# Context rows of a cross-attention: given with exchanged axes and centred in place, instead of transposed on TensorE

## The chip, the cores and the metric

The kernel runs on one core of one Trainium2 chip. The metric is the time of one execution on the device in microseconds (us), as a median of several runs. Beside it there is one profiled execution, whose trace gives every row shown here. The host arranges inputs before the launch; that is not in the time.

## The reference

Three layers are added to `x` (4 batches of 128 rows of 512); the change touches the first, an attention of these 128 latents over 2048 context rows per batch:

```python
ctx = layer_norm(context, ln_ctx_g, ln_ctx_b)        # (x - mean) * rsqrt(var + 1e-5) * g + b, over 512 columns
q = lat @ Wq                                         # lat: the latents, normalised in the same way
k, v = jnp.split(ctx @ Wkv, 2, axis=-1)              # 16 heads of 64
k = apply_rope(k, cos, sin)
attn = softmax(clip(q @ k.T * 64 ** -0.5, -11, 11))
out = attn @ v                                       # then @ Wo + bo, added to x
```

A linear attention and a mixture of experts follow. All of it is float32; products are made of high and low parts (hi*hi + hi*lo + lo*hi).

## The kernel before

`prepare` computes the queries of all batches and splits the weights of keys and values into high and low parts, piece by piece (eight pieces, two buffers). It also does the first four of the 64 context row tiles (128 rows each). A barrier ends it. `attend` is a loop over 128 steps t, each for a pair of heads: 32 steps per batch, in four chunks of 512 context rows, eight steps each. The body of one batch is written out once and looped over. Each engine has its own `step(b, t)`, whose order is the order of its queue; semaphores tie the engines together. TensorE's step is: scores of pair t - 4, values of step t, keys of step t (12 products of 512 columns each), and the weighing of the values by the probabilities of pair t - 5. ScalarE copies the scores, splits probabilities and values and takes exponents; VectorE adds scores (L794), rotates keys (L762 to L776) and takes low parts; GpSimd clips (L617) and makes low parts of probabilities (L610), of rotated keys (L629) and of context rows (L156). Rotated keys are copied by DMA from SBUF to SBUF (`store_keys`, L586), four copies every two steps, and the queries of a pair are loaded from DRAM (L528). All of these DMAs are issued by SyncE, in order.

The context rows of a later chunk are prepared on the way, one tile in each odd step (`row_tile_of`). SyncE loads it with rows on partitions (L565). VectorE takes its mean and variance (L107 to L115), GpSimd the power -1/2 (L120), VectorE normalises it (L126), since mean and factor are one number per partition. TensorE transposes its four blocks against an identity (L134) in the middle of the values' products, after waiting for the normalised rows, and writes a bank of PSUM that it shares with the weighed sums. ScalarE scales and shifts the four blocks out of PSUM (L711; in `prepare` VectorE, L142), now with columns on partitions, takes the high part (L149), and GpSimd the low one (L156). Values and keys wait for the low parts. The order of VectorE in an odd step is: rotate, add weighed sums, normalise (L126), take scores (L794), low values (L803), statistics.

## Time and profile before

| | |
|---|---|
| median of 3 runs | 1433.24 us (1431.34 to 1437.6) |
| profiled execution | 1435.82 us |
| its span in the trace | 1434.1 us |
| TensorE busy | 1383.0 us, 96% |
| VectorE busy | 853.2 us, 59% |
| ScalarE busy | 796.5 us, 56% |
| GpSimd busy | 829.8 us, 58% |
| HBM read and written | 132.67 and 16.78 MB |

The span is that of the instructions on the core; the time of the execution has 1.7 us around it. Busy time of TensorE counts the overlapping parts of pipelined products once; the duration of a single product is longer than its place in the queue, so places are read from starts. An idle time in square brackets stands ahead of the instruction named, with what ended it. L12 is line 12 of the kernel, and "q" behind an engine's name means its queue (waits and issues).

### The profile page before, as it was taken

The page shows a single profiled execution, that of the slowest core. Times are in us where ns is not written, and L with a number is a line of the kernel's source. Part 1 is how long each engine was busy: PE and PEld are TensorE (multiplying, and loading weights), DVE is VectorE, ACT ScalarE, POOL GpSimd, SP SyncE. Part 2 cuts the span into 40 slices and gives each one's busy share as a digit, 9 for nine tenths or more (in the row PEclk, how much of TensorE's full clock was granted, in tenths as well). Part 3 has the DMA queues.
Part 4 walks back from the last instruction along what each step waited for, and adds up shares of the span by engine and source line. Part 5 has one row for each costly group of instructions (what it writes and reads, how often), then busy time and mean ns, then how long its engine had stood idle before and what let it go on. Part 6 is the DMA issues. An engine that isn't in the chain of part 4 may idle for free. (4 is left out here: it accounts for less than half of the span.)

```text
span 1434.1 us, 25248 instructions
## 1 busy us (share of the span) xinstructions
PE 1383.0 (96%) x8758; PEld 1131.0 (79%) x8758; DVE 853.2 (59%) x1422; ACT 796.5 (56%) x1237; POOL 829.8 (58%) x721
## 2 busy tenths in 40 slices
PE   5899999999999999999999999999999999999998
PEld 3578888888788888888888888888888666766654
DVE  6356566566565656665565566665556556657554
ACT  3356666666565666665566666666645512446552
POOL 3267767777676777776677776777766343200002
PEclk9999999999999999999999999999999999899999
DMA  6567676667566666756666766766687545469994
GB/s 240 185 114 131 117 133 107 123 121 133 107 124 123 119 125 115 136 113 122 123 119 111 129 118 130 139 110 117 101 187 133 142 147 183 167 236 360 356 354 141
DMA packets 115267, 218.44 MB, mean 152 GB/s; under 512 B 13360, under 2 KB 49200, under 8 KB 108976
## 3 DMA queue, kind: packets, MB, share of 16 engines
q1 hardware_dynamic: 111968, 209.00, 64.9%
q0 software_dynamic: 1280, 4.20, 0.9%
q10 hardware_dynamic: 1872, 3.41, 0.6%
q8 instruction: 77, 1.26, 0.4%
q14 instruction: 70, 0.57, 0.2%
HBM read 132.67 MB, written 16.78 MB: 104 GB/s over the span
## 5 line engine op out<-in xcount | busy, mean ns | idle before, releaser
L610 POOL TENSOR_TENSOR p_parts<-probs,p_parts 128x512 fp32r<-128x512 f32 x256 | 341.3, 1352 | 249.5 <-ACT p_parts L668 249.5
L668 ACT ACTIVATE p_parts<-probs 128x512 fp32r<-128x512 f32 x256 | 147.7, 625 | 239.0 <-PE banks L978 231.1
L794 DVE TENSOR_TENSOR probs<-banks,probs 128x1024 f32<-128x1024 f32 x128 | 156.7, 1224 | 147.6 <-ACT probs L674 147.6
L698 ACT ACTIVATE probs<-probs 128x1024 f32<-128x1024 f32 x128 | 135.8, 1061 | 144.4 <-POOL probs L617 144.4
L930 PE MATMUL banks<-wv_hi,x_hi 128*128 128x512 f32 x512 | 208.5, 407 | 4.8 <-PEq L170 4.8
L931 PE MATMUL banks<-wv_lo,x_hi 128*128 128x512 f32 x512 | 203.0, 396 | 0.0
L945 PE MATMUL banks<-x_hi,wk_hi 128*128 128x512 f32 x512 | 201.8, 394 | 0.0
L932 PE MATMUL banks<-wv_hi,x_lo 128*128 128x512 f32 x512 | 201.7, 394 | 0.0
L947 PE MATMUL banks<-x_hi,wk_lo 128*128 128x512 f32 x512 | 199.6, 390 | 0.0
L946 PE MATMUL banks<-x_lo,wk_hi 128*128 128x512 f32 x512 | 199.3, 389 | 0.0
L974 PE MATMUL banks<-p_parts,v_hi 128*65 128x128 f32 x1024 | 191.7, 224 | 0.0
L978 PE MATMUL banks<-p_parts,v_hi 128*65 128x128 f32 x1024 | 191.1, 223 | 0.0
L976 PE MATMUL banks<-p_parts,v_lo 128*64 128x128 f32 x1024 | 191.0, 223 | 0.0
L617 POOL TENSOR_SCALAR probs<-probs 128x1024 f32<-128x1024 f32 x128 | 153.6, 1200 | 27.5 <-DVE probs L794 19.2
L914 PE MATMUL banks<-queries,keys 128*128 128x256 f32 x1024 | 150.6, 290 | 6.4 <-issue 5.5
L976 PEld LDWEIGHTS banks<-p_parts,v_lo 128*64 128x64 f32 x1024 | 138.8, 136 | 11.8 <-issue 0.6
L974 PEld LDWEIGHTS banks<-p_parts,v_hi 128*65 128x65 f32 x1024 | 139.5, 136 | 5.2 <-issue 0.5
L978 PEld LDWEIGHTS banks<-p_parts,v_hi 128*65 128x65 f32 x1024 | 139.1, 136 | 0.0
L914 PEld LDWEIGHTS banks<-queries,keys 128*128 128x128 f32 x1024 | 130.8, 191 | 7.6 <-issue 5.7
L674 ACT ACTIVATE probs<-banks 128x1024 f32<-128x1024 f32 x128 | 128.9, 1007 | 9.2 <-PE banks L914 8.7
L932 PEld LDWEIGHTS banks<-wv_hi,x_lo 128*128 128x128 f32 x512 | 97.3, 190 | 22.0
L930 PEld LDWEIGHTS banks<-wv_hi,x_hi 128*128 128x128 f32 x512 | 97.9, 191 | 20.3 <-issue 5.6
(296 smaller groups left out, 2682.4 us busy)
## 6 DMA issues: line engine op xcount, KB each, us to landing
queries<-q_scratch SPq DMA_DIRECT2D x256, 128.0 KB, 6.0
keys<-wo_room SPq DMA_DIRECT2D x128, 256.0 KB, 5.6
keys<-turned_odd SPq DMA_DIRECT2D x128, 256.0 KB, 5.6
row_room<-in_ctx SPq DMA_DIRECT2D x64, 256.0 KB, 6.2
wo_room<-in_down SPq DMA_DIRECT2D x10, 1024.0 KB, 8.0
late_room<-in_gate SPq DMA_DIRECT2D x8, 1024.0 KB
gate_raw<-in_up SPq DMA_DIRECT2D x8, 1024.0 KB, 9.8
up_raw<-in_gate SPq DMA_DIRECT2D x7, 1024.0 KB, 9.1
```

The costliest lines, as they stand in the source:

```text
L610: nc.gpsimd.tensor_tensor(p_parts[:, 1, j, :], probs[:, pair % 2, j, :], p_parts[:, 0, j, :].bitcast(F32), ALU.subtract).then_inc(p_lo_rea ...
L794: nc.vector.tensor_tensor(mine, ps_s[:, :, :, 0, :].rearrange("p j i n -> p (j i) n"), mine, ALU.add).then_inc(s_taken, 1)
L914: mm = nc.tensor.matmul(ps_s[:, j, i], keys[:, slot, 2 * (pair % 2) + j, i * P:(i + 1) * P], queries[:, pair % QUERY_SLOTS, j], start=True ...
L930: nc.tensor.matmul(out, x_hi[:, buf, k, cols], wv_hi[:, k, heads], start=(k == 0), stop=False)
L931: nc.tensor.matmul(out, x_hi[:, buf, k, cols], wv_lo[:, k, heads], start=False, stop=False)
L932: mm = nc.tensor.matmul(out, x_lo[:, buf, k, cols], wv_hi[:, k, heads], start=False, stop=(k == KT - 1))
L945: nc.tensor.matmul(ps_k, wk_hi[:, k, cols], x_hi[:, buf, k, :], start=(k == 0), stop=False)
L946: nc.tensor.matmul(ps_k, wk_hi[:, k, cols], x_lo[:, buf, k, :], start=False, stop=False)
L947: mm = nc.tensor.matmul(ps_k, wk_lo[:, k, cols], x_hi[:, buf, k, :], start=False, stop=(k == KT - 1))
L974: nc.tensor.matmul(sums[:, j, :], v_hi[:, i, 2 * m + j, :], p_parts[:, 0, j, cols], start=(i == 0), stop=False)
L976: nc.tensor.matmul(sums[0:DHEAD, j, :], v_lo[:, i, 2 * m + j, :], p_parts[:, 0, j, cols], start=False, stop=False)
L978: mm = nc.tensor.matmul(sums[:, j, :], v_hi[:, i, 2 * m + j, :], p_parts[:, 1, j, cols], start=False, stop=(i == ROW_TILES - 1))
```

## The change

The host gives the context a second time, as `ctx_t`, in tiles whose axes are exchanged: 512 columns on the partitions (four blocks), 128 rows along them. This copy is loaded into `xt`. The rows with rows on partitions are still loaded (`row_in`), for the statistics alone. Mean and factor are now needed as a row of 128 numbers, the same on every partition: SyncE stores `mean_var` (128 partitions by mean and factor) in DRAM (`row_stats`), waits in its queue until it has landed, and loads it back spread over all partitions (`load_spread`). VectorE subtracts the mean and multiplies by the factor in place (`centre_rows`, both inputs in SBUF, the spread row repeated for the four blocks), behind the taking of the scores. ScalarE scales and shifts in place, behind the exponents. TensorE's transposes go, with its waits for them. Statistics are taken two steps earlier than before, and seven tiles are measured in `prepare`, where four are centred. Space is regrouped: `xt` takes two of the three parts of `row_room`, `bo` gets a place of its own under later tensors.

```diff
--- before.py
+++ after.py
...
-def normalise_row_tile(nc, r, dve, tile, slot):
-    wait(dve, r["rstd_ready"], tile + 1)
-    nc.vector.tensor_scalar(r["row_in"][:, slot, :], r["row_in"][:, slot, :], r["mean_var"][:, slot, 0:1],
-                            r["rstd"][:, slot:slot + 1], ALU.subtract, ALU.mult).then_inc(r["row_ready"], 1)
...
-def transpose_row_tile(nc, r, pe, tile, slot):
-    wait(pe, r["row_ready"], tile + 1)
-    wait(pe, r["full_ready"], tile)
-    for k in range(KT):
-        tr = nc.tensor.transpose(r["ps_tr"][:, k, :], r["row_in"][:, slot, k * P:(k + 1) * P], r["ident"][:])
-    tr.then_inc(r["tr_ready"], 1)
...
+def load_turned(nc, r, d, sp, tile, slot, landed):
+    sp.dma_start(r["xt"][:, slot], d["ctx_t"][tile]).then_inc(landed, 16)
+
+
+def load_spread(sp, to, stats, landed):
+
+
+    whose = stats.rearrange("r w -> (r w)").unsqueeze(0).to_broadcast([P, stats.shape[0] * 2])
+    sp.dma_start(to.rearrange("p n w -> p (n w)"), whose).then_inc(landed, 16)
...
@@ -231,8 +210,7 @@
                 sp.dma_start(x_in[:, b, :], d["x"][b]).then_inc(x_landed[b], 16)
             for n, to in (("lat_g", lat_g), ("lat_b", lat_b), ("ctx_g", keep["ctx_g"]), ("ctx_b", keep["ctx_b"])):
                 sp.dma_start(to[:], d[n]).then_inc(small_landed, 16)
-            for i in range(ROW_TILES):
-                load_row_tile(nc, rows, sp, i, i)
+            sp.dma_start(rows_early[:, 0:ROW_TILES], rows["source"][0:ROW_TILES].rearrange("t p d -> p t d")).then_inc(rows["pair_landed"][0], 16)
...
+            def store_stats(first, last, n):
+                sp.wait_ge(rows["rstd_ready"], n + 1)
+                sp.dma_start(d["row_stats"][first:last].rearrange("t p w -> p t w"), row_mv[:, first:last]).then_inc(rows["stat_stored"], 16)
+                sp.wait_ge(rows["stat_stored"], 16 * (n + 1))
+
             load_piece(0)
+            sp.dma_start(rows["xt"], d["ctx_t"][0:ROW_TILES].rearrange("t p k n -> p t k n")).then_inc(rows["spread_landed"], 16)
+            store_stats(0, ROW_TILES, 0)
+            load_spread(sp, spread_early[:].rearrange("p t n w -> p (t n) w"), d["row_stats"][0:ROW_TILES].rearrange("t p w -> (t p) w"), rows["spread_landed"])
             load_piece(1)
             for m in range(PAIRS):
                 if m + 2 < len(pieces):
                     load_piece(m + 2)
+                if m == 0:
+                    sp.dma_start(rows_early[:, ROW_TILES:MEASURED],
+                                 rows["source"][ROW_TILES:MEASURED].rearrange("t p d -> p t d")).then_inc(rows["pair_landed"][1], 16)
                 if m == 1:
                     load_angles(sp, d, keep, 0, 0)
-                if m >= 4 and m < 7:
-                    load_row_tile(nc, rows, sp, m, m - ROW_TILES)
+                    sp.dma_start(rows["row_in"][:, MEASURED % 2], rows["source"][MEASURED]).then_inc(rows["pair_landed"][1], 16)
+                if m == 5:
+                    store_stats(ROW_TILES, MEASURED, 1)
+                    load_spread(sp, rows["spread"][:].rearrange("p t n w -> p (t n) w"), d["row_stats"][ROW_TILES:EARLY].rearrange("t p w -> (t p) w"), rows["spread_landed"])
+                    for tile in range(ROW_TILES, EARLY):
+                        sp.wait_ge(rows["lo_ready"], tile - ROW_TILES + 1)
+                        load_turned(nc, rows, d, sp, tile, tile % ROW_TILES, rows["pair_landed"][tile % 2])
                 sp.wait_ge(q_lo, m + 1)
                 sp.dma_start(d["q_scratch"][m], q_stage[:, m % 2].rearrange("p b w n -> p b (w n)").bitcast(F32)).then_inc(q_stored[m % 2], 16)
+            for i in range(2):
+                sp.wait_ge(rows["pair_landed"][i], PAIR_BASE[i])
+            sp.wait_ge(rows["spread_landed"], SPREAD_BASE)
...
+
+            def rows_variance(first, last):
+                for i in range(first, last):
+                    stat = nc.vector.bn_aggr(row_mv[:, i, :], row_stats[:, i, :])
+                link(stat)
+                nc.vector.tensor_scalar(row_var[:, first:last], row_mv[:, first:last, 1], EPS, None, ALU.add).then_inc(rows["var_ready"], 1)
+
+            def centre_rows(tile):
+                if tile == 0:
+
+                    dve.wait_ge(rows["spread_landed"], 32)
+                mine = rows["xt"][:, tile]
+                for w, op in ((0, ALU.subtract), (1, ALU.mult)):
+                    link(nc.vector.tensor_tensor(mine, mine, spread_early[:, tile, :, w].unsqueeze(1).to_broadcast([P, KT, P]), op))
+                for k in range(KT):
+                    out = nc.vector.tensor_scalar(mine[:, k, :], mine[:, k, :], keep["ctx_g"][:, k:k + 1], keep["ctx_b"][:, k:k + 1],
+                                                  ALU.mult, ALU.add)
+                out.then_inc(rows["full_ready"], 1)
...
-                    tile = row_tile_of(b, t + 5)
+                    tile = row_tile_of(b, t + 3)
                     if tile is not None:
-                        wait(sp, rows["tr_ready"], b * ROWS_OF_BATCH + (tile - 3))
-                        slot = tile % ROW_TILES
-                        sp.dma_start(rows["row_in"][:, slot, :],
-                                     rows["source"][b * ROWS_OF_BATCH + tile]).then_inc(rows["row_landed"][slot], 16)
+                        whole = b * ROWS_OF_BATCH + tile
+                        wait_alone(sp, rows["lo_ready"], whole - 3)
+                        load_turned(nc, rows, d, sp, whole, tile % ROW_TILES, rows["pair_landed"][tile % 2])
+                        if row_tile_of(b, t + 7) is not None:
+                            wait_alone(sp, rows["stats_ready"], whole + 1 - MEASURED)
+                            sp.dma_start(rows["row_in"][:, tile % 2, :],
+                                         rows["source"][whole + 2]).then_inc(rows["pair_landed"][tile % 2], 16)
                     for pair in (t - 3, t - 2):
                         if exists(b, pair) and exists(b, t - 2):
                             load_queries(b, pair)
+                tile = row_tile_of(b, t + 2) if t >= 1 else None
+                if tile is not None:
+                    whole = b * ROWS_OF_BATCH + tile
+                    if not isinstance(whole, int) or whole >= MEASURED:
+                        wait_alone(sp, rows["rstd_ready"], STATS + whole + 1 - MEASURED)
+                        sp.dma_start(d["row_stats"][whole], rows["mean_var"][:, tile % ROW_TILES, :]).then_inc(rows["stat_stored"], 16)
+                        wait_alone(sp, rows["stat_stored"], 16 * (STATS + whole + 1 - MEASURED))
+                        wait_alone(sp, rows["spread_landed"], SPREAD_BASE + 16 * (whole - EARLY))
+                    wait_alone(sp, rows["xt_ready"], 2 * (whole - 1 - ROW_TILES))
+                    load_spread(sp, rows["spread"][:, tile % 2], d["row_stats"][whole], rows["spread_landed"])
...
-                tile = row_tile_of(b, t + 1) if t >= 2 else None
+                tile = row_tile_of(b, t + 3) if t >= 2 else None
                 if tile is not None:
-                    row_tile_power(nc, rows, pool, b * ROWS_OF_BATCH + tile, tile % ROW_TILES)
+                    mine = rows["mean_var"][:, tile % ROW_TILES, 1:2]
+                    wait(pool, rows["var_ready"], b * ROWS_OF_BATCH + (STATS + tile + 1 - MEASURED))
+                    nc.gpsimd.tensor_tensor(mine, rows["var_eps"][:, tile % ROW_TILES:tile % ROW_TILES + 1],
+                                            rows["minus_half"][:, 0:1], ALU.pow).then_inc(rows["rstd_ready"], 1)
...
+                exponents(b, t - SCORE_LAG)
+                rope_high(b, t, 1)
                 tile = row_tile_of(b, t)
                 if tile is not None:
-                    whole = b * ROWS_OF_BATCH + tile
-                    wait(act, rows["tr_ready"], whole + 1)
-                    wait(act, rows["lo_ready"], whole - 1)
+                    mine = rows["xt"][:, tile % ROW_TILES]
+                    wait(act, rows["xt_ready"], 2 * (b * ROWS_OF_BATCH + (tile - ROW_TILES + 1)))
                     for k in range(KT):
-                        out = nc.scalar.activation(rows["x_full"][:, tile % 2, k, :], rows["ps_tr"][:, k, :], ACT.Identity,
+                        out = nc.scalar.activation(mine[:, k, :], mine[:, k, :], ACT.Identity,
                                                    bias=rows["ctx_b"][:, k:k + 1], scale=rows["ctx_g"][:, k:k + 1])
                     out.then_inc(rows["full_ready"], 1)
-                exponents(b, t - SCORE_LAG)
-                rope_high(b, t, 1)
...
+            def centre_rows(b, tile):
+                whole, slot = b * ROWS_OF_BATCH + tile, tile % ROW_TILES
+                if tile >= EARLY:
+                    wait(dve, rows["pair_landed"][tile % 2], landings(b, tile))
+                    wait(dve, rows["spread_landed"], SPREAD_BASE + 16 * (whole + 1 - EARLY))
+                mine = rows["xt"][:, slot]
+                mean, factor = (rows["spread"][:, tile % 2, :, w].unsqueeze(1).to_broadcast([P, KT, P]) for w in range(2))
+                nc.vector.tensor_tensor(mine, mine, mean, ALU.subtract).then_inc(rows["xt_ready"], 1)
+                wait(dve, rows["xt_ready"], 2 * (whole - ROW_TILES) + 1)
+                nc.vector.tensor_tensor(mine, mine, factor, ALU.mult).then_inc(rows["xt_ready"], 1)
...
+            def measure_rows(b, tile):
+                whole, slot, turn = b * ROWS_OF_BATCH + tile, tile % ROW_TILES, tile % 2
+
+                if tile > MEASURED:
+                    wait(dve, rows["pair_landed"][turn], landings(b, tile - 2))
+                n = whole - MEASURED + 1
+                var = rows["mean_var"][:, slot, 1:2]
+                nc.vector.bn_stats(rows["stats"][:, slot, :], rows["row_in"][:, turn, :]).then_inc(rows["stats_ready"], 1)
+                wait_alone(dve, rows["stats_ready"], n)
+                nc.vector.bn_aggr(rows["mean_var"][:, slot, :], rows["stats"][:, slot, :]).then_inc(rows["mean_ready"], 1)
+                wait(dve, rows["mean_ready"], n)
+                nc.vector.tensor_scalar(rows["var_eps"][:, slot:slot + 1], var, EPS, None, ALU.add).then_inc(rows["var_ready"], 1)
...
+                take_scores(b, t - SCORE_LAG)
                 tile = row_tile_of(b, t)
                 if tile is not None:
-                    normalise_row_tile(nc, rows, dve, b * ROWS_OF_BATCH + tile, tile % ROW_TILES)
-                take_scores(b, t - SCORE_LAG)
+                    centre_rows(b, tile)
                 combine(b, t, 1)
                 values_low(b, t - 1)
                 if not last:
                     finish(b, t - VALUE_LAG - 1)
-                tile = row_tile_of(b, t + 2) if t >= 1 else None
-                if tile is not None and t % 2 == 1:
-                    whole = b * ROWS_OF_BATCH + tile
-                    measure_row_tile(nc, rows, dve, whole, tile % ROW_TILES, b * CHUNKS + (tile // ROW_TILES + 1))
-                    wait_alone(dve, rows["stats_ready"], whole + 1)
-                    row_tile_variance(nc, rows, dve, whole, tile % ROW_TILES)
+                tile = row_tile_of(b, t + 4) if t >= 1 else None
+                if tile is not None:
+                    measure_rows(b, tile)
...
-                    tile = row_tile_of(b, pair + VALUE_LAG)
-                    if tile is not None:
-
-                        wait(pe, rows["full_ready"], b * ROWS_OF_BATCH + tile + 1)
...
-                tile = row_tile_of(b, t)
-                if tile is not None:
-
-                    if exists(b, t - VALUE_LAG - 1):
-                        wait(pe, o_added, b * BSTEPS + (t - VALUE_LAG))
-                    transpose_row_tile(nc, rows, pe, b * ROWS_OF_BATCH + tile, tile % ROW_TILES)
...
+    d["row_stats"] = nc.dram_tensor("row_stats", (BATCH * CTX // P, P, 2), F32).ap()
...
-        keep["row_in"] = room[:, 0:2, :].rearrange("p a (t n) -> p (a t) n", n=DIM)
-        keep["x_full"] = room[:, 2, :].rearrange("p (a t n) -> p a t n", a=2, n=P)
+        keep["xt"] = room[:, 0:2, :].rearrange("p a (t k n) -> p (a t) k n", k=KT, n=P)
+        keep["row_in"] = room[:, 2, :].rearrange("p (t n) -> p t n", n=DIM)
...
+        "ctx_t": a["ctx_1024"].reshape(BATCH * CTX // P, P, KT, P).transpose(0, 3, 2, 1),
...
```

## Rows read from the trace of the kernel before

**Rows 1.** The page: busy time, share of the span, instructions of each engine.
```profile
PE 1383.0 (96%) x8758; PEld 1131.0 (79%) x8758; DVE 853.2 (59%) x1422; ACT 796.5 (56%) x1237; POOL 829.8 (58%) x721
```

**Rows 2.** Table by windows: PE, PEld, DVE, ACT, POOL busy, clock, DMA share, GB/s.
```profile
700.00:957.00 257.00, 257.00 (x1834) 223.20 (x1832) 156.96 (x275) 161.89 (x267) 189.64 (x158) 1.00 0.67 122
```

**Rows 3.** TensorE's waits, 57 to 1130 us: sum, times, longest.
```profile
PE banks L134 <- DVE row_room L126: 2.3, 3, 1.1
PE banks L914 <- DMA keys<-wo_room: 0.8, 1, 0.8
```

**Rows 4.** TensorE's timeline, 500 to 532 us: start, us, instructions.
```profile
506.13 1.17 PE L914 MATMUL banks<-queries,keys 128*128 128x256 f32 x8
...
508.53 0.60 PE L134 MATMUL banks<-ident,row_room 128*128 128x128 f32 x4
...
514.52 1.16 PE L914 MATMUL banks<-queries,keys 128*128 128x256 f32 x8
...
522.46 1.16 PE L914 MATMUL banks<-queries,keys 128*128 128x256 f32 x8
```

**Rows 5.** VectorE's timeline, the same stretch.
```profile
506.83 0.55 DVE L126 TENSOR_SCALAR row_room<-row_room,mean_var,rstd 128x512 f32<-128x512 f32 x1
508.49 1.22 DVE L794 TENSOR_TENSOR probs<-banks,probs 128x1024 f32<-128x1024 f32 x1 [1.11 <-ACT probs L674]
...
513.28 0.69 DVE L765 TENSOR_TENSOR turned_odd<-banks,wo_room 128x512 f32<-128x512 f32 x1 [1.89 <-PE banks L947]
...
518.02 0.69 DVE L776 TENSOR_TENSOR turned_odd<-turned_odd 128x512 f32<-128x512 f32 x1
```

**Rows 6.** ScalarE's timeline, the same stretch.
```profile
514.78 1.16 ACT L668 ACTIVATE p_parts<-probs 128x512 fp32r<-128x512 f32 x2 [2.77 <-PE banks L978]
```

**Rows 7.** GpSimd's timeline, the same stretch.
```profile
509.88 1.04 POOL L617 TENSOR_SCALAR probs<-probs 128x1024 f32<-128x1024 f32 x1
...
515.49 2.67 POOL L610 TENSOR_TENSOR p_parts<-probs,p_parts 128x512 fp32r<-128x512 f32 x2 [3.31 <-ACT p_parts L668]
518.27 1.35 POOL L617 TENSOR_SCALAR probs<-probs 128x1024 f32<-128x1024 f32 x1
...
523.43 2.65 POOL L610 TENSOR_TENSOR p_parts<-probs,p_parts 128x512 fp32r<-128x512 f32 x2 [0.33 <-ACT p_parts L668]
```

**Rows 8.** SyncE's queue, the same stretch: DMA issues.
```profile
517.88 5.29 SPq L586 DMA_DIRECT2D keys<-turned_odd  x4
...
524.28 2.81 SPq L528 DMA_DIRECT2D queries<-q_scratch  x4
```

**Rows 9.** Landings: the copy issued at 522.62; L586; L556; then SyncE's longest wait.
```profile
keys<-turned_odd SPq DMA_DIRECT2D x1, 256.0 KB, 6.8
...
DMA to landing us min/median/max: 3.9/5.6/8.9
...
DMA to landing us min/median/max: 1.6/4.3/6.4
...
SPq L556 <- DVE attn L820: 48.2, 12, 4.1
```

**Rows 10.** Before the loop: a window as in rows 2, then timelines of SyncE, VectorE, GpSimd, TensorE.
```profile
0.00:20.00 20.00, 4.81 (x18) 3.92 (x19) 13.54 (x41) 5.71 (x12) 5.16 (x15) 1.00 0.72 263
...
6.92 15.59 SPq L242 DMA_DIRECT2D w_raw<-in_wv  x3
...
24.77 0.69 DVE L372 TENSOR_TENSOR q_stage<-a_ps,q_stage 128x512 fp32r<-128x512 f32 x1 [1.53 <-ACT q_stage L297]
...
28.86 0.69 DVE L372 TENSOR_TENSOR q_stage<-a_ps,q_stage 128x512 fp32r<-128x512 f32 x1 [2.13 <-ACT q_stage L297]
...
14.57 2.08 POOL L120 TENSOR_TENSOR rstd<-var_eps,minus_half 128x1 f32<-128x1 f32 x4 [2.50 <-DVE var_eps L115]
...
53.75 1.05 POOL L120 TENSOR_TENSOR rstd<-var_eps,minus_half 128x1 f32<-128x1 f32 x2 [6.34 <-DVE var_eps L115]
...
55.14 0.77 PE L930 MATMUL banks<-wv_hi,x_hi 128*128 128x512 f32 x1 [4.82 <-PEq L170]
```

102 lines of the change are left out of this document (46 added, 56 removed).

## Prediction

> **What bounds the kernel now.** I read the page's busy shares first: TensorE is busy 96% of the span, no other engine for computing over 60% [rows 1]. A share is a mean over stages, so next the table by windows: in the attention loop TensorE is busy 257.0 of 257.0 us at full clock, with the DMA engines at 0.67 [rows 2]. Then TensorE's own waits from 57 to 1130 us: beside the turns of the batch loop, 2.3 us in three waits of the row transposes for VectorE's normalised rows, 0.8 us for keys [rows 3]. So in the loop (55 to about 1128 us) each us taken from TensorE's queue is a us of the span, as long as nothing else comes late. TensorE's timeline gives the period: scores begin at 506.13, 514.52 and 522.46, so an odd step (with transposes) takes 8.39 us and an even one 7.94 [rows 4]. The stages behind the attention are not touched.
>
> **The change, part by part.**
>
> *Transposes.* Removed: four per row tile, 60 tiles in the loop. The four take 0.60 us by themselves, but overlap their neighbours; what the queue gives back is the difference of the two steps, 8.39 - 7.94 = 0.45 us [rows 4]. 60 x 0.45 = 27.0 us. Bounds: 0.44 (another pair of steps reads the same to 0.01) and 0.60, if nothing of it overlapped; I take 0.45, the direct reading, and hold 26 to 28. Their three waits, 2.3 us, go with them [rows 3]; what is late next behind them is the score's wait for keys, below, so I count 2. Together 29 us. The 16 transposes of the stage before the loop are under other work there and count nothing.
>
> *VectorE in the loop.* Removed per tile: the normalisation, 0.55 us, that stood in the shadow of the wait for ScalarE's copied scores (1.11 us idle behind it). Added, and moved behind the taking of the scores: two operations with both inputs in SBUF. The nearest row is the sum L776, 0.69 us [rows 5]; lower bound is that, upper bound twice it, since one input is repeated over k and read every other element, which no row shows; I take 0.69, for its size and its places are the same. So the odd step has 1.4 to 2.8 us more between taking the scores (ends 509.71) and the next keys (513.28, behind 1.89 us of idle) [rows 5]. With the odd step 0.45 us shorter, 1.4 us fit in the idle time to within 0.1 us; 2.8 would run 1.3 us over into the even step, where the rotation is wanted only about 3.8 us after the step begins, and the scores still find 1.1 us idle. Cost nothing; the cover is that idle time.
>
> *ScalarE.* The four scalings now read SBUF and stand behind the exponentials. ScalarE has 2.77 us of idle before the next split of the probabilities [rows 6]. The centring ends at about 511.3, the scalings 1.5 us later, 1.5 us before ScalarE is wanted. Nothing.
>
> *GpSimd.* It has the same operations. In the even step it is nearly full: 0.33 us idle before the next split [rows 7], and that step isn't shortened. Beside L776, GpSimd's clip takes 1.35 us, without such a neighbour 1.04 [rows 5, 7]: an operation of VectorE with two SBUF inputs holds GpSimd back by 0.31 us. The new ones will do that in the odd step, two times, 0.6 us, where GpSimd has 3.3 us of idle [rows 7]. The Trainium skill (SBUF — State Buffer, Who interferes with whom) says more: such an instruction and a GpSimd one that reads SBUF exclude each other, and the later "fully blocks". The trace's 0.31 us is in line with a short remainder of such a lock, not with a whole one. This makes a part of rival B.
>
> *The queue of SyncE.* This is the part that can turn the sign. New per tile: a load of the turned tile (256 KB, beside the old one), a store of 1 KB in pieces of 8 bytes, a wait in SP's queue until it has landed, and a load that spreads it over the partitions (128 KB). Before, SP issues four key copies from 517.88 to 523.17, then a row tile, then from 524.28 four query loads in 2.81 us [rows 8]. The new wait comes right behind the last key copy, with which it shares the queue. That copy lands 6.8 us after its issue at 522.62; key copies take 3.9 to 8.9, the small stores of attention results 1.6 to 6.4 [rows 9]. I take X = 5.6 us for the store, landing with the last keys at 529.4; bounds 1.6 and 8.9. Queued behind that wait: the spread load, the turned tile and the row tile at about 0.5 us each (four query loads take 2.8, 0.7 each, with two register waits), and the queries, so SP is free at 523.7 + 5.6 + 4.3 = 533.6, once in four periods 1.2 later for the angles. The next keys are due at 517.88 + 15.9 = 533.8: it just fits. Queries landing 6 us behind their issue (531 for the first pair) are in time for 538. More bytes: 384 KB each 15.9 us, 1.5 us at the 263 GB/s that the first 20 us moved [rows 10]; the DMA share goes from 0.67 to some 0.8.
> The keys are the tight end: the last land at 529.4, the scores that need them begin one period behind 514.52, at 530.4: 1.0 us of slack. If the first key copy goes out over about 2 us late, it joins the other three and all come late. In the periods with angles and with stores of attention results (some 30 of 60) I allow 0.1 us on average: 3 us. Bounds 0 and 0.5 us in all 60, 30 us, of which the upper end is a rival.
>
> *Before the loop.* Here the round trip is on the path. Now the bytes up to both first weight pieces, 5.2 MB, land by about 20 us at 263 GB/s. After: the turned tiles (1 MB) come ahead, SP then waits for powers (made at 14.57 now, in one operation about 17 then), for the store (behind 5.8 MB, so 22 us), issues the spread load and only then the second weight piece, now among the issues from 6.92 on [rows 10]. It lands at about 28, its split ends at 30, and the first query split follows, 24.8 before: 5 us late. VectorE then has 1.4 us more per m for four m (two 0.69 operations), which fits into the 2.13 us idle between them [rows 10]; three early measurements move forward. At m = 5 another store and wait stands ahead of the sixth query store: 3 to 5 us, partly beside others; against that the power of two tiles at the end (1.05 us, until 54.8, the last thing before the loop starts at 55.14) goes away [rows 10]. Sum: +5 + 2 to 4 - 1, I take +6.5; bounds 0 (all made up by the 1.5 to 2.1 us idle of each m) and +13 (both trips in full).
>
> **Sum.** 27 + 2 - 3 - 6.5 = 19.5 us less. The profiled execution had 1435.82 us (span 1434.1); its after is 1416.3. The median before is 1433.24, 2.6 us under it, so the median after is 1433.24 - 19.5 = 1413.7 us.
>
> **Rivals.**
> A. *The start hides it.* The idle of each m absorbs the late start and keys stay in time: -29, 1404 to 1406. For it: idle of about 2 us in each of four m. Against: VectorE needs 1.4 of these for itself. Chance 0.12.
> B. *Keys a little late in every period.* SP's order or the longer queue lets the last keys land 0.3 to 0.5 us after they are wanted: 18 to 30 us, of which 3 are in the sum: 1429 to 1441, no change. For it: 1.0 us of slack is all there is. Against: the keys' own issue hangs on ScalarE and GpSimd, whose even step doesn't change. Chance 0.12. A form of it is a full block between the two engines: if each new operation waits out one of GpSimd of 1.3 us, the odd step of VectorE ends some 2.6 us later, the even step of GpSimd and the last key copy about 2 us, 1 us over the slack; in half the periods that is 30 us, 1444. It is the skill's rule named above. It has 0.04 of B's chance, since the trace shows 0.31 us.
> C. *Slower: SP's queue becomes the bound.* Place: the wait for the landing of the 8-byte pieces. SP can be 2.4 us later than worked out before keys pile up, and then 1.0 us more before scores wait: from X = 9.0 us each further us costs 60 us. At X = 10: 1414 + 60 = 1474 us; break-even is at X = 9.3. For it: 128 pieces of 8 bytes to DRAM, which no row shows. Against: no key copy lands later than 8.9, no small store later than 6.4 [rows 9], and around batch ends SP already waits about 4 us at this place, 12 times, while TensorE's waits for keys are 0.8 us in all [rows 3, 9]. Chance 0.11. The Trainium skill (DMA: Bandwidth & Descriptors, Specifications) asks for 512 B or more per piece, below which the engine reads, modifies and writes; it gives no time for 8-byte pieces. By its fixed cost of about 2 us per transfer (section Anatomy of one DMA) the store would be X = 2, and the 3 us for keys would leave the sum: an estimate of 1411.
> That the transposes don't leave TensorE's queue can't be, by the diff.
>
> **Chances.** Forecast 0.65, A 0.12, B 0.12, C 0.11. Range 1403 to 1432: it takes in the forecast's bounds (1413.7 less 3 and 6.5 for a start and keys that cost nothing, 1404; plus 6.5 and some us of keys, 1424) and part of B. About 0.5% (7 us) is what a measurement of this kernel can tell from no change: faster by more (under 1426) 0.79, within 0.09, slower 0.12.
>
> **What would show it.** Both steps of TensorE at 7.94 us; no wait of L914 for keys or queries; the store's landing near 5.6 us and SP through its queries before the next rope halves are ready; TensorE's first L930 at about 61 to 62, not 55; VectorE's new operations at 0.69 us; centring never waiting for the spread load. Wrong if TensorE shows regular waits at L914, or if VectorE's rotation starts late enough that L945 waits.

## The result, and the profile after it

The changed kernel takes 1497.25 us (median, 1491.59 to 1502.6), the kernel before 1432.29 in the same comparison: a ratio of 1.045, 95% interval 1.042 to 1.0481, so slower by 4.5%. The forecast was 1413.7 us, with a range of 1403 to 1432. The profiled execution took 1498.11 us, its span 1495.2.

The span can be cut at two marks: the first matmul of the values ends the start, the first of the output projection ends the attention loop. All kernels of this study, profiled executions, us (tiles of rows in the loop: 60; e7 has one trip more in 57 of them):

| kernel | start | loop | rest | span | median | ratio to before [95%] |
|---|---|---|---|---|---|---|
| before | 55.1 | 1060.0 | 319.0 | 1434.1 | 1432.3 | |
| after | 71.8 | 1105.2 | 318.2 | 1495.2 | 1497.3 | 1.045 [1.042, 1.048] |
| e1_no_wait | 70.1 | 1051.6 | 322.9 | 1444.6 | 1438.8 | 1.003 [1.001, 1.005] |
| e2_no_round_trip | 70.1 | 1033.4 | 319.9 | 1423.4 | 1425.2 | 0.993 [0.990, 0.996] |
| e3_no_turned_load | 70.2 | 1068.8 | 322.8 | 1461.8 | 1459.9 | 1.017 [1.012, 1.022] |
| e4_wait_later | 70.7 | 1052.4 | 317.1 | 1440.2 | 1435.5 | 1.001 [0.999, 1.003] |
| e6_start_and_later | 65.1 | 1052.7 | 320.0 | 1437.8 | 1437.8 | 1.003 [1.001, 1.005] |
| e7_two_trips | 72.8 | 1288.5 | 320.8 | 1682.1 | 1682.8 | 1.173 [1.169, 1.178] |
| e8_reordered | 64.1 | 1041.3 | 320.4 | 1425.8 | 1426.1 | 0.994 [0.992, 0.997] |
| e9_loop_order | 71.9 | 1039.1 | 317.6 | 1428.6 | 1429.3 | 0.995 [0.994, 0.997] |
| e10_wide_pieces | 71.5 | 1043.8 | 319.9 | 1435.2 | 1436.4 | 1.003 [1.000, 1.005] |
| e13_weights_first | 59.9 | 1037.0 | 317.5 | 1414.4 | 1416.6 | 0.987 [0.985, 0.989] |

So of the 61.1 us that the change costs in the profiled executions (65.0 by the medians), 16.7 lie before the loop, 45.2 in it, and -0.8 behind it. A run's ratio is taken to the kernel before as timed beside it on the same chip, at 1434.3 to 1434.7 us for e1 to e13.

The page of the kernel after, busy time of each engine (before: [rows 1]), and the window of the loop (columns as in [rows 2]):

```profile
PE 1372.0 (92%) x8502; PEld 1116.7 (75%) x8502; DVE 952.0 (64%) x1481; ACT 806.8 (54%) x1237; POOL 882.7 (59%) x716
...
700.00:957.00 257.00, 243.06 (x1690) 209.40 (x1689) 174.43 (x279) 155.71 (x254) 193.94 (x151) 0.99 0.74 140
```

TensorE, full in this window before, now idles 13.9 of 257 us, and no other engine took its place: VectorE is busy 174 us of it, GpSimd 194. That looks like a chain of waits, not like an engine that has too much to do; the experiments decide it. TensorE's waits from 57 to 1170 us name their place (engine, tile and line; what released it; us in all, times, longest), against [rows 3]:

```profile
PE banks L965 <- issue: 36.9, 26, 4.1
PE banks L981 <- PEq L145: 20.1, 1, 20.1
PE banks L965 <- DMA keys<-wo_room: 19.3, 14, 2.6
PE banks L965 <- DMA keys<-turned_odd: 5.4, 8, 1.2
```

L965 (L914 before) is the score matmul; L981 is the first matmul of the values, whose one wait is for the barrier that ends the start. A step between two scores without a wait takes some 7.93 us now, odd or even, where the odd one took 8.39 [rows 4]: the transposes are gone. But some 49 of 128 scores wait. "Issue" means that the profile shows no releaser, so it must be read from the timelines. SyncE's queue and the scores of TensorE in one stretch ("..." stands for the loads of `xt`, `row_in` and the angles):

```profile
539.63 0.40 SPq L593 DMA_DIRECT2D row_stats<-mean_var  x1
546.98 0.34 SPq L119 DMA_DIRECT2D spread_rows<-row_stats  x1
...
548.62 2.82 SPq L543 DMA_DIRECT2D queries<-q_scratch  x4
551.55 3.62 SPq L614 DMA_DIRECT2D keys<-turned_odd  x4
555.42 0.39 SPq L593 DMA_DIRECT2D row_stats<-mean_var  x1
563.99 0.34 SPq L119 DMA_DIRECT2D spread_rows<-row_stats  x1
...
565.63 2.82 SPq L543 DMA_DIRECT2D queries<-q_scratch  x4
...
569.89 2.84 SPq L614 DMA_DIRECT2D keys<-wo_room  x4
572.99 0.39 SPq L593 DMA_DIRECT2D row_stats<-mean_var  x1
```
```profile
555.80 1.19 PE L965 MATMUL banks<-queries,keys 128*128 128x256 f32 x8 [1.50 <-issue]
563.75 1.16 PE L965 MATMUL banks<-queries,keys 128*128 128x256 f32 x8
572.66 1.19 PE L965 MATMUL banks<-queries,keys 128*128 128x256 f32 x8 [0.84 <-issue]
```

Two things are to be seen. First, SyncE goes round here almost without a pause of its own: from store to store 15.79 and 17.57 us, of which 7.35 and 8.57 go by until the store's landing lets it issue the spread load; the rest, 8.4 and 9.0 us, are nearly all issues. The four key copies, paced by ScalarE and spread over 5.29 us before [rows 8], go out at 569.89 in 2.84: they had been ready and waited for SyncE. Over the loop the four take 3.2 us (median of 64 sets, 5.3 before). Two steps of TensorE are 15.9 us, so SyncE has no time left where the landing takes over about 7 us. Second, the queries. They are sent behind the wait, the first pair of copies from 548.62 to about 549.9, and these two land 4.8 and 6.3 us after their issue, the later one at about 555.7; the odd score starts at 555.80, 1.50 us after TensorE was free. The next pair, issued from 565.63, is there at about 572.5, and the score starts at 572.66. So "issue" is a wait for queries here. Taken over the loop, odd scores wait 30.1 us in 25 places, even ones, which use a new set of keys, 32.2 us in 24. The landings confirm the split: ahead of each waiting odd score the queries land last, 0.09 to 0.23 us before it starts, with the keys there for over 8 us. Ahead of the waiting even ones the keys land last; only in two of them, with 7.5 us, had they been there for 1.0 and 3.4 us, and the same two scores wait 5.5 us in the kernel before.

SyncE's slack is its own wait at the key copies for ScalarE, which makes them. Its two rows before (57 to 1130 us) and after (57 to 1170 us), 508.8 us in 125 waits against 90.8 in 61:

```profile
SPq L586 <- ACT wo_room L693: 259.6, 61, 11.5
SPq L586 <- ACT turned_odd L693: 249.2, 64, 7.9
```
```profile
SPq L614 <- ACT wo_room L724: 55.0, 30, 7.6
SPq L614 <- ACT turned_odd L724: 35.8, 31, 5.7
```

The landing itself (us from issue, least, median, most) of the store L593, and SyncE's waits for it from 57 to 1170 us (L65 is the helper that waits; where it has no row, the wait stands at the next issue, L119):

```profile
DMA to landing us min/median/max: 4.9/7.5/10.8
```
```profile
SPq L65 <- DMA row_stats<-mean_var: 332.3, 48, 9.7
SPq L119 <- DMA row_stats<-mean_var: 76.7, 9, 10.1
```

SyncE spends 409 us of the span in 57 waits for 1 KB each. In all 57 the store lands behind the last of the four key copies issued ahead of it, by 0.15 to 2.0 us (median 0.77); that copy is issued 0.84 us before the store and takes 7.5 us itself (median).

### The profile page after: what moved, and what is told of

The parts are those of the page before. It is cut to its first block and busy times, and to the rows that moved or that the text cites. A ratio compares the mean times of both kernels' runs of the same rounds, so it can differ in the third digit from the quotient of the medians.

```text
span 1495.2 us, 25506 instructions
## 1 busy us (share of the span) xinstructions
PE 1372.0 (92%) x8502; PEld 1116.7 (75%) x8502; DVE 952.0 (64%) x1481; ACT 806.8 (54%) x1237; POOL 882.7 (59%) x716
## 5 line engine op out<-in xcount | busy, mean ns | idle before, releaser
L638 POOL TENSOR_TENSOR p_parts<-probs,p_parts 128x512 fp32r<-128x512 f32 x256 | 350.1, 1389 | 180.1 <-ACT p_parts L699 179.8
L645 POOL TENSOR_SCALAR probs<-probs 128x1024 f32<-128x1024 f32 x128 | 173.9, 1358 | 89.3 <-DVE probs L824 86.9
L981 PE MATMUL banks<-wv_hi,x_hi 128*128 128x512 f32 x512 | 204.0, 398 | 20.1 <-PEq L145 20.1
L965 PE MATMUL banks<-queries,keys 128*128 128x256 f32 x1024 | 155.3, 296 | 62.7 <-issue 36.9
L965 PEld LDWEIGHTS banks<-queries,keys 128*128 128x128 f32 x1024 | 133.4, 194 | 70.3 <-issue 56.4
L981 PEld LDWEIGHTS banks<-wv_hi,x_hi 128*128 128x128 f32 x512 | 99.1, 194 | 37.4 <-issue 20.9
L131 POOL TENSOR_TENSOR x_lo<-row_room,x_hi 128x512 fp32r<-128x512 f32 x64 | 109.0, 1704 | 16.2 <-ACT x_hi L124 16.2
```

Source lines behind the costliest of these rows:

```text
L638: nc.gpsimd.tensor_tensor(p_parts[:, 1, j, :], probs[:, pair % 2, j, :], p_parts[:, 0, j, :].bitcast(F32), ALU.subtract).then_inc(p_lo_rea ...
L645: nc.gpsimd.tensor_scalar(mine, mine, CLIP / SCALE, -CLIP / SCALE, ALU.min, ALU.max).then_inc(clipped, 1)
L965: mm = nc.tensor.matmul(ps_s[:, j, i], keys[:, slot, 2 * (pair % 2) + j, i * P:(i + 1) * P], queries[:, pair % QUERY_SLOTS, j], start=True ...
L981: nc.tensor.matmul(out, x_hi[:, buf, k, cols], wv_hi[:, k, heads], start=(k == 0), stop=False)
```

## The experiments

Theory (C of the prediction): SyncE's queue, stretched by the wait for the store, is the bound in the loop. Rivals: more bytes to move; VectorE and GpSimd in each other's way (B's lock form); the start alone. The first three kernels each take one thing away, e4 moves one.

**e1_no_wait**: store and spread load stay, the wait is for the store of the tile before, which landed long ago.

```diff
+wait_alone(sp, rows["stat_stored"], 16 * (STATS + whole - MEASURED))
 sp.dma_start(d["row_stats"][whole], rows["mean_var"][:, tile % ROW_TILES, :]).then_inc(...)
-wait_alone(sp, rows["stat_stored"], 16 * (STATS + whole + 1 - MEASURED))
...
-load_spread(sp, rows["spread"][:, tile % 2], d["row_stats"][whole], rows["spread_landed"])
+load_spread(sp, rows["spread"][:, tile % 2], rows["source"][whole][0:1, 0:2 * P], rows["spread_landed"])
...
```

> The changed kernel, but SP doesn't wait for the landing of the mean and factor of this tile (only, ahead of the store, for that of the tile before), and the spread load reads 1 KB of the context instead, so the rows are centred with other numbers: the result isn't the attention's. All DMAs and all work of the engines stay. Theory W (the wait in SP's queue makes queries and keys late): the loop loses its 70 us of waits, about 1430 us; the start, 16.7 us later than before, stays. Theory B (the bytes of the added loads make keys late): 1490. Theory C (VectorE's two operations and GpSimd hold each other up): 1490.

Measured 1438.8 us, the loop 53.6 us shorter than in the changed kernel, with all its bytes and all its work on VectorE and GpSimd. Both of these rivals had 1490. Waits of odd scores: none; even ones still wait 22.7 us in 14 places, so not all of the 70 us went.

**e2_no_round_trip**: in the loop no store, no wait, no spread load.

```diff
-sp.dma_start(d["row_stats"][whole], rows["mean_var"][:, tile % ROW_TILES, :]).then_inc(...)
-wait_alone(sp, rows["stat_stored"], 16 * (STATS + whole + 1 - MEASURED))
-wait_alone(sp, rows["spread_landed"], SPREAD_BASE + 16 * (whole - EARLY))
-load_spread(sp, rows["spread"][:, tile % 2], d["row_stats"][whole], rows["spread_landed"])
...
 (ahead of the turned load)
+wait_alone(sp, rows["xt_ready"], 2 * (whole - 1 - ROW_TILES))
 (VectorE, ahead of the centring)
-wait(dve, rows["spread_landed"], SPREAD_BASE + 16 * (whole + 1 - EARLY))
```

> The changed kernel without store, wait for landing and spread load in the loop: every tile there is centred with the mean and factor of tiles 4 and 5, so the result isn't the attention's. The turned loads and the engines' work stay. Theory W: as the run without the wait, 1425 to 1430 us. Theory B: a third of the added bytes goes, 1475. Theory C: 1490.

Measured 1425.2 us, the loop 1033.4: 26.6 less than before, where 27.0 were forecast for the transposes. The two new operations of VectorE, the four scalings from SBUF and the turned load are all still in it, so together they cost nothing that can be seen. Its window, to be held against [rows 2] and the window above:

```profile
700.00:957.00 257.00, 256.43 (x1814) 222.08 (x1813) 189.97 (x298) 166.31 (x273) 209.70 (x161) 1.00 0.68 143
```

This gives the price of the round trip in the loop: 1105.2 - 1033.4 = 71.8 us. The waits at the scores make 54 us of it (60.9 against 6.8, from the first score on). In the ten windows of 100 us from 100 to 1100 the granted clock is 0.988 on average in the changed kernel and 0.996 here, some 8 us; the last step before a wait shows 8.09 us, the wait itself not counted, where a free one shows 7.93, some 48 times, another 8.

**e3_no_turned_load**: the turned tile isn't loaded, the round trip stays.

```diff
-load_turned(nc, rows, d, sp, whole, tile % ROW_TILES, rows["pair_landed"][tile % 2])
...
 (VectorE, ahead of the centring)
+wait(dve, rows["lo_ready"], whole - 3)
```

> The changed kernel without the turned tile's load in the loop (256 KB less per tile, one issue less); old contents are centred again, so the result isn't the attention's. Store, wait and spread load stay. Theory W: SP's chain is 0.5 us shorter per tile, 1480 to 1490 us. Theory B: two thirds of the added bytes go, 1450. Theory C: 1490.

Measured 1459.9 us, the loop 1068.8, 36.4 us shorter than in the changed kernel. The 1480 to 1490 of the theory is missed, and the time lies nearer to the 1450 of the rival with the bytes. That rival alone doesn't hold, since e1 and e2 carry the same load at 1051.6 and 1033.4 us; but beside the wait the load costs more than the theory said. SyncE has one issue less, some 0.6 us, and the store lands at a median of 6.9 us instead of 7.5; SyncE's waits for it stay the largest (303.3 us in 48, the other form 68.6 in 9). Read as the same closed loop, shorter by these two amounts, 1.2 us in 57 tiles would give up to 68 us, and 36.4 were measured; so the size isn't explained, and which of the two does more wasn't taken apart.

**e4_wait_later**: the same store at the same place, but its wait and the spread load stand behind the queries of the next even step.

```diff
 sp.dma_start(d["row_stats"][whole], rows["mean_var"][:, tile % ROW_TILES, :]).then_inc(...)
-wait_alone(sp, rows["stat_stored"], 16 * (STATS + whole + 1 - MEASURED))
-wait_alone(sp, rows["spread_landed"], SPREAD_BASE + 16 * (whole - EARLY))
...
 (behind load_queries of step t, even)
+tile = row_tile_of(b, t + 1) if t >= 2 else None
+    wait_alone(sp, rows["stat_stored"], 16 * (STATS + whole + 1 - MEASURED))
+    wait_alone(sp, rows["spread_landed"], SPREAD_BASE + 16 * (whole - EARLY))
+    load_spread(sp, rows["spread"][:, tile % 2], d["row_stats"][whole], rows["spread_landed"])
```

> The changed kernel, all of its work kept, but in the loop the wait for the landing and the spread load stand behind the query loads of the next even step instead of right behind the store. The store has the time of the other loads' issues to land. Theory W: most of the 70 us of waits in the loop go, about 1430 us, with the late start left. Theory B: 1490. Theory C: 1490.

Measured 1435.5 us, the loop 1052.4. The store lands no sooner (5.3, 7.4, 9.3), so its time alone costs nothing; what cost was standing ahead of queries and keys. Odd scores wait nowhere now, even ones 22.2 us in 12. TensorE's waits, 57 to 1170 us:

```profile
PE banks L971 <- DMA keys<-wo_room: 10.0, 7, 2.3
PE banks L971 <- issue: 8.6, 2, 4.4
PE banks L971 <- DMA keys<-turned_odd: 3.7, 3, 1.6
```

The two "issue" waits are those of the same two scores as above, which every kernel here has. Of the other ten, seven come once in four periods, behind the loads of angles. That SyncE's wait for `stats_ready` ahead of the queries (150.6 us in 34 waits) adds to them is argued, not shown; e8 and e9 act on both.

**e7_two_trips**: the store and its wait twice, one behind the other.

```diff
 wait_alone(sp, rows["stat_stored"], ...)
+sp.dma_start(d["row_stats_again"][whole], rows["mean_var"][:, tile % ROW_TILES, :]).then_inc(rows["stat_stored"], 16)
+wait_alone(sp, rows["stat_stored"], 32 * (STATS + whole + 1 - MEASURED) - 16 * STATS)
```

> The changed kernel with a second store of the same 1 KB and a wait for it, behind the first wait, in each of 57 tiles. Alone in the queue such a store should land in 2 to 3 us. If SP's chain of wait, loads and key copies is the bound of the loop, each of 57 periods gets 2 to 3 us longer: 1610 to 1670 us. If the store's bytes or the engines were the cause: about 1500.

Measured 1682.8 us, above the 1610 to 1670 expected; the loop is 183.3 us longer, 3.2 for each of 57 tiles. The second store, alone in the queue, lands in (least, median, most):

```profile
DMA to landing us min/median/max: 2.9/3.4/4.5
```

So about each us that SyncE waits longer is a us of the loop, in every tile: the queue is the bound, and not only near it. SyncE's own waits for ScalarE at the key copies fall from 61 to 17. It falls on the odd scores (57 to 1170 us; over the whole loop it is 168.2 us in 53):

```profile
PE banks L967 <- issue: 154.1, 48, 6.4
```

Over the loop TensorE is busy 1099.5 of 1288.5 us, and 1039.5 of 1105.2 in the changed kernel: 123 us of the 183 are waits, 60 are slower work. The granted clock is at its lower level (1.2 GHz) for 172 us of this loop and for 33 of the changed kernel's. So part of the slope may be the clock's; no run separates the two.

The 3.4 us are also the price of 128 pieces of 8 bytes with nothing ahead of them in their queue; the first store, right behind the key copies, takes 7.8 in the same run.

**e10_wide_pieces**: the store writes 128 pieces of 512 bytes (a constant tile) instead of 128 of 8; wait and spread load stay where they are, and the load reads what was stored.

```diff
-sp.dma_start(d["row_stats"][whole], rows["mean_var"][:, tile % ROW_TILES, :]).then_inc(rows["stat_stored"], 16)
+sp.dma_start(d["wide_stats"][whole], keep["ident"][:]).then_inc(rows["stat_stored"], 16)
...
```

> The changed kernel, but what is stored and waited for are 128 pieces of 512 B (64 KB of constants) in place of 128 pieces of 8 B, and the spread load reads those, so the result isn't the attention's. If the small pieces make the landing slow: it falls from 7.5 us to some 5 and the time to about 1450. If the store lands late because it rides behind the key copies in the same queue: 7.5 to 8 us and 1497 or a little more.

Its landing, against 4.9/7.5/10.8:

```profile
DMA to landing us min/median/max: 4.5/6.1/9.6
```

With 64 times the bytes the store lands 1.4 us sooner, and the loop takes 1043.8 us, 61.4 less than the changed kernel, or 1.1 us per tile. Both expectations are missed: the landing lies between them, the time (1436.4) is below both. Not all of the 1.4 us is the size of the pieces. The store lands 0.20 us behind the last key copy now, and 0.77 before: 0.6 us are its own. The last key copy takes 6.8 us instead of 7.5, with the four issued over a longer time: 0.7 us, a part of which comes back from the loop that is relieved. The other 6.1 us are time in which the store stands behind the four key copies, and its own trip. The Trainium skill (DMA: Bandwidth & Descriptors, Specifications) asks for pieces of 512 B or more; this case agrees, 7.5 against 6.1 us, of which 0.6 are the store's own.

**e6_start_and_later**: e4, and before the loop the second piece of the weights ahead of the turned tiles and of the first wait; the second store one m earlier, its wait one m later than in the changed kernel (m counts the eight rounds of the start).

```diff
+load_piece(1)
 ...
-load_piece(1)
 ...
-if m == 5:
+if m == 4:
+    (second store, no wait)
+if m == 6:
+    sp.wait_ge(rows["stat_stored"], 32)
```

> The kernel with the wait moved behind the queries (1435.5 us, its loop begins at 70.7 us), and before the loop: the second weight piece is issued ahead of the turned tiles and of the first wait; the second store goes out one m earlier, its wait one m later. If the late start comes from SP's two waits there: the loop begins 7 to 10 us earlier, at 61 to 63, about 1427 us. If it comes from VectorE's longer work there: no change.

In the profiled executions the loop starts 5.6 us earlier than in e4, but the medians don't show it: 1437.8 (9 runs, ratio 1.0005 to 1.0045) against 1435.5 (9 runs, 0.999 to 1.003). The start is 65.1 where 61 to 63 was expected, the time 1437.8 where it was 1427. The kernels ran on different chips. This one stays inconclusive.

**e8_reordered**: e6, and in the loop row_in's load behind the queries, the angles in an odd step; before the loop the second trip behind the sixth query store, VectorE's work on the latents first, and the scalings of the first four tiles on ScalarE.

```diff
 (even step, ahead of the queries)
-wait_alone(sp, rows["stats_ready"], whole + 1 - MEASURED)
-sp.dma_start(rows["row_in"][:, tile % 2, :], rows["source"][whole + 2])...
 (behind the queries)
+wait_alone(sp, rows["stats_ready"], whole + 1 - MEASURED)
+sp.dma_start(rows["row_in"][:, tile % 2, :], rows["source"][whole + 2])...
...
-if t % STEPS == 2 and exists(b, t - 2 + STEPS):
+if t % STEPS == 3 and exists(b, t - 3 + STEPS):
```

> All work kept. In the loop: the wait behind the queries as before, and now the row tile's load behind the queries too, since it waits for VectorE's statistics, and the angles in the odd step behind the store, where SP has nothing to do. Before the loop: as in the run beside it, the second round trip wholly behind the sixth query store, VectorE does the latents ahead of the first row statistics, and ScalarE scales the first four tiles. If SP's order alone makes keys late: the loop takes 1035 to 1040 us, as without the round trip (1033), and the start falls to 58 to 60: about 1412 us. If the bytes make keys late too: a loop of 1050 and 1425 us.

1426.1 us (ratio 0.992 to 0.997); start 64.1, loop 1041.3. The loop is 1.3 us above the range of the first theory and well under the 1050 of the rival, so nearly all of the loop's loss was the order of SyncE's queue. The start missed 58 to 60, and with the loop that is most of the 14 us between 1426 and the 1412 expected. It is the first version under the kernel before that leaves nothing out.

**e9_loop_order** has the loop of e8 and the start of the changed kernel.

> The changed kernel with only the loop's part of e8_reordered: wait and load of the spread means behind the queries of the next even step, the load of row_in behind the queries, the angles in an odd step; the start is left as in the changed kernel. Theory 'SyncE's queue in the loop and the start are two separate costs that add': the start stays at 70 to 72 us, the loop takes 1041 to 1043 us as in e8, and the time is 1431 to 1434 us, 5 to 8 us above e8. Rival 'they share a cause', as e6 and e4 beside each other could suggest (start 5.6 us earlier in the profile, time not shorter): the time comes out within 2 us of e8, at 1425 to 1428.

Start 71.9, loop 1039.1, median 1429.3. It lies between the two expectations, 3.2 us above e8, and not 5 to 8: of the 7.8 us that e8 starts earlier, 2.2 are lost in its loop and 2.8 behind it in the profiled executions. Why, isn't known; the scores wait 14.1 us in e8 and 12.3 in e9 (from the first score on).

**e13_weights_first** is e8 with one exchange ahead of the loop, on GpSimd:

```diff
 for i in range(ROW_TILES):
-    row_tile_low(nc, rows, pool, i, 0, i)
     if i % 2 == 0:
         weights_low(i + 2)
+    row_tile_low(nc, rows, pool, i, 0, i)
```

> The kernel of e8_reordered with one exchange ahead of the loop: GpSimd makes the low parts of the weights before the low parts of its row tile, not behind them. In e8 the loop began at 64.1 us (71.8 in the changed kernel, 55.1 in the kernel before) and took 1041.3 us. Theory 'the start is now GpSimd': the two late pieces of the weights (issued at 36.3 and 47.6 us) waited for GpSimd's row work; ordered the other way the loop begins at 57 to 60 us, the loop stays at 1041 to 1042, and the time falls from 1426.1 to 1419 to 1422 us, a ratio of 0.990 to 0.992. Rival 'the start is the round trip': the second trip of the row statistics sets the start whatever GpSimd does first; the loop begins at 63 to 65 us and the time stays at 1425 to 1427. Second rival 'only moved': the row parts come late instead, and the loop begins at 66 us or later, 1428 or more.

1416.6 us, ratio 0.985 to 0.989 to the kernel before: 1.3% faster. The start is 59.9 us, as the first theory said, the loop 1037.0, 4 less than it said, and the time 2.4 us under its range. Against e9, on the same chip, start 12.0 earlier and median 12.7 lower, so here the start adds in full. SyncE's order in it, one period:

```profile
540.79 6.50 SPq L623 DMA_DIRECT2D keys<-turned_odd  x4
547.53 0.39 SPq L599 DMA_DIRECT2D row_stats<-mean_var  x1
548.22 0.35 SPq L112 DMA_DIRECT2D row_room<-in_ctx_t  x1
548.67 2.86 SPq L546 DMA_DIRECT2D queries<-q_scratch  x4
552.39 0.34 SPq L589 DMA_DIRECT2D row_room<-in_ctx  x1
555.61 0.33 SPq L119 DMA_DIRECT2D spread_rows<-row_stats  x1
556.62 7.08 SPq L623 DMA_DIRECT2D keys<-wo_room  x4
```

The store still takes 7.8 us to land (median), but behind it the turned tile, the queries and row_in are sent; SyncE is left with 3 us of waiting here (85.0 us in 41 waits over the loop, for 409 in 57), and the key copies are paced by ScalarE again (7.08 us for four, not 2.84).

## Why the prediction was wrong, point by point

The step that failed is the one where SyncE's wait for the store "just fits": it was priced at 3 us of late keys, and it cost 71.8 us in the loop. By the profiled spans the forecast was 19.5 us less and the result 61.1 more, 80.6 apart: 68.8 are this wait, 10.2 the start, 2.4 the transposes and their waits, -0.8 the rest.

- **Transposes**: right. 27.0 us forecast, 26.6 measured (e2 against before), and both steps at 7.92 to 7.93 us. The 2 us more for their waits didn't come: those 2.3 us went, but the scores' waits grew, from 6.3 us to 9.1 in e2.
- **VectorE**: right in what matters. Both operations hide (e2). Their sizes over the 60 tiles, durations in ns (least, median, most), and one case of the second beside GpSimd:

```profile
L880 DVE TENSOR_TENSOR row_room<-row_room,spread_rows x60: 680/682/978, 71.8 to 1083.6; 128x512 f32<-128x512 f32 x60
...
L882 DVE TENSOR_TENSOR row_room<-row_room,spread_rows x60: 691/1410/1661, 72.5 to 1084.3; 128x512 f32<-128x512 f32 x60
...
560.02 1.41 DVE L882 TENSOR_TENSOR row_room<-row_room,spread_rows 128x512 f32<-128x512 f32 x1
...
559.54 1.34 POOL L645 TENSOR_SCALAR probs<-probs 128x1024 f32<-128x1024 f32 x1 [1.92 <-DVE probs L824]
```

  L880 is the 0.69 us taken. L882 takes 0.72 us more where it meets GpSimd's clip: the clip runs from 559.54 to 560.88, L882 starts at 560.02 and ends at 561.43, 0.55 us behind it. In 57 of the 60 tiles it is so; the two L882 without a GpSimd operation beside them take 0.69. So the block between the two engines is nearer to a whole one than the 0.31 us of [rows 5, 7] suggested. The Trainium skill (SBUF — State Buffer, Who interferes with whom) says that such a VectorE operation and a GpSimd one that reads SBUF contend for ports under an exclusive lock, and that the order of issue decides which of them blocks; 1.41 against 0.69 for the later one agrees. But it costs nothing: e2 has both operations and loses nothing by them.
- **ScalarE, GpSimd**: right. A scaling from SBUF takes 479 ns against 456 from PSUM; GpSimd's clip is slowed by 0.3 us (1.34 against 1.04), all of it hidden.
- **SyncE's queue**: here the forecast failed, at three terms.
  1. *The landing.* X = 5.6 us was taken, the median of the key copies; it is 7.5, inside the bounds of 1.6 and 8.9. The store goes out behind four key copies of 256 KB in its queue and has pieces of 8 bytes: 3.4 us alone (e7), 6.1 in wide pieces behind the copies (e10), 7.5 as it is. The text had it land with the last keys, which is nearly so (0.77 us behind them), but it took the median of all key copies for X. The last copy of each four takes 6.7 us before, as the one in [rows 9] with 6.8; less 0.84 and plus 0.77 us that makes 6.6, and the last copy itself went to 7.5 in the changed kernel. The estimate of X = 2 from the fixed cost of about 2 us in the Trainium skill (DMA: Bandwidth & Descriptors, Anatomy of one DMA) is under even the least landing of the store alone, 2.9 us; that section measures transfers that GpSimd issues, and these are SyncE's.
  2. *The threshold.* C was held to decide from X = 9.0, counted for the keys alone. The queries stand behind the same wait, and their being in time was checked at X = 5.6 alone. By the prediction's own numbers, they go out 1.5 us behind the landing, the second copy of the first pair at about 523.7 + 5.6 + 1.5 + 0.7 = 531.5, and with 6 us to landing they are there at 537.5, wanted at 538: 0.5 us of slack, where [rows 8] left some 7 before. So "in time for 538" was true at X = 5.6 and false from 6.1 on, and no rival had a price for it. (In the changed kernel queries take 4.5 us by the median, 6.0 before, but 6.3 and 6.15 in the two late pairs of the stretch.) They make half of the waits, 30.1 of 62.3 us.
  3. *The closed loop.* Lateness was priced as once in a while ("3 us"). But SyncE's wait is in the loop of its own issues: X and 8.4 to 9.0 us against a period of 15.9, so from X = 7 or so nothing is left to catch up with, and each further us is paid in every tile (e7: 3.2 us per tile for 3.4 us of landing). At X = 5.6 it "just fits" in the prediction, with 0.2 us (533.6 against 533.8). Rival C had this mechanism and the slope of 60 us per us right; with its threshold at 7 (the loop) or 6.1 (the queries) instead of 9.0 it gives, at X = 7.5, 1414 + 60 x 0.5 to 60 x 1.4 = 1444 to 1498. These thresholds are fitted after the result, and the late start comes on top. It had a chance of 0.11.
- **Before the loop**: +6.5 us forecast, bounds 0 and 13; it was +16.7, outside them. In the kernel after SyncE's queue shows (start, us):

```profile
6.12 0.68 SPq L228 DMA_DIRECT2D row_room<-in_ctx_t  x1
...
19.24 0.39 SPq L224 DMA_DIRECT2D row_stats<-e_mean_var  x1
23.72 0.34 SPq L119 DMA_DIRECT2D spread_early<-row_stats  x1
24.10 1.83 SPq L220 DMA_DIRECT2D w_raw<-in_wv  x2
...
56.06 0.79 SPq L224 DMA_DIRECT2D row_stats<-e_mean_var  x1
61.51 0.34 SPq L119 DMA_DIRECT2D spread_rows<-row_stats  x1
61.89 0.91 SPq L112 DMA_DIRECT2D row_room<-in_ctx_t  x2
62.84 8.41 SPq L248 DMA_DIRECT2D q_scratch<-q_stage  x3
```

  The first trip is near the forecast: the store out at 19.24, back at 23.7 (22 said), the second weight piece out at 24.10; the first query split of VectorE starts at 31.85 for 24.77 before [rows 10], 7.1 us late where 5 were said. The term that failed is the rest, "+2 to 4 - 1", which was about 10. The second trip (5.5 us) stands ahead of three query stores, the last of which leaves at 71, and the VectorE operations were held up beside GpSimd: in two of the four tiles the four scalings (L350) take 3.03 us instead of 1.11, while GpSimd makes the low parts of weights. The bounds took both trips in full but let the idle time of each m take up all else. How the 10 us split between these wasn't taken apart. Most of them can be had back: e6 (order of SyncE) begins the loop at 65.1, e8 (the scalings on ScalarE, too) at 64.1, and e13, with GpSimd's pieces of weights ahead of the row work, at 59.9, 4.8 behind the kernel before.
- **What would show it**: TensorE's regular waits at the scores were named as the sign of a wrong forecast, and they are what the profile shows.

In sum: -26.6 (transposes, as forecast) + 71.8 (round trip in the loop; 3 less 2 forecast) + 16.7 (start; 6.5 forecast) - 0.8 = 61.1 us.

## What to carry to other kernels

A wait in a DMA queue's program is priced by all that stands behind it up to the point where the queue comes round again: write down the slack of each transfer behind it, queries as well as keys, and sum the issues plus the landing against the period; where nothing is left, each us of landing is a us per tile. Take the landing of a small store from a small store at the same place in the queue; where there is none, from the last transfer ahead of it in that queue (it landed behind that one in all 57 tiles), not from the median of all. And put other work that is ready between the store and its wait: here this alone, at an unchanged landing, brought 62 us (e4), and the order of the whole queue and of the start, with the first scalings moved to ScalarE, turned 4.5% slower into 1.3% faster (e13). Whether the store would land sooner from another engine's queue, without key copies ahead of it, wasn't run.

## What the runs showed of the hardware

- A store of 128 pieces of 8 bytes to DRAM lands 3.4 us after its issue with nothing ahead of it (2.9 to 4.5), 7.5 right behind four copies of 256 KB on the same queue (4.9 to 10.8), always behind the last of them (by 0.15 to 2.0); 128 pieces of 512 bytes in the same place land in 6.1, 0.20 behind it.
- An operation of VectorE with both inputs in SBUF goes from 0.69 to 1.41 us when GpSimd is in the midst of one of 1.34 us (57 of 60 tiles; the two with no GpSimd operation beside them take 0.69); GpSimd's next one, 1.29 us alone, took 1.73 beside such operations.
- TensorE's granted clock was 0.97 to 0.98 in five of the ten windows of 100 us in the changed kernel, and in two of ten in e2, where it hardly waits; the other windows are at 1.00, the level of 2.4 GHz. In e7, where TensorE waits at 72 scores, it was 0.94 over the span.
